# A gated cross-attention block: the second token half of the last batch gets a PSUM bank of its own, ScalarE scales it and VectorE adds it

## What is computed

```
x = x + tanh(g_xattn) * xattn(layernorm(x), ctx)          # attention over the context
x = x + tanh(g_ffn)   * ffn(layernorm(x))

ffn(x): gate = gelu(fp8(x) @ fp8(w_gating[0]))
        up   =      fp8(x) @ fp8(w_gating[1])
        return fp8(gate * up) @ fp8(w_linear)
```

## Time and profile before

| what | value |
|---|---|
| median of 3 runs | 49.52 us (49.23 to 51.98) |
| the profiled execution | 49.34 us |
| its span in the trace | 47.5 us |
| around the span | 1.84 us |
| PE busy | 41.6 us, 87% |
| DVE busy | 34.7 us, 73% |
| ACT busy | 29.5 us, 62% |
| POOL busy | 16.8 us, 35% |

### The profile page before, as it was taken

The page is one execution under the profiler, slowest core; times in us unless marked ns, Lnnn a source line. Parts: engine busy times, 40 slices in busy tenths (PEclk is TensorE's granted clock), DMA queues, the critical chain, the costliest instruction groups (busy, mean ns, idle before and its releaser), DMA issues.

```text
span 47.5 us, 841 instructions
## 1 busy us (share of the span) xinstructions
PE 41.6 (87%) x246; PEld 28.6 (60%) x246; DVE 34.7 (73%) x110; ACT 29.5 (62%) x67; POOL 16.8 (35%) x35
## 2 busy tenths in 40 slices
PE   3998999963999999998999999999999999999000
PEld 1317788833787888863435556665645888895000
DVE  0101099999798979899999991787669977999700
ACT  0902947299798799755599749775557495463000
POOL 3204994039999641600610170000000059802300
PEclk9999999999999999999999999999999999999999
DMA  0499999999999960000000000000000001460092
GB/s 0 79 365 326 317 367 369 195 203 203 170 114 104 106 61 1 0 0 21 0 0 0 0 0 0 0 0 7 0 0 0 0 14 64 163 215 0 0 340 102
DMA packets 3460, 4.64 MB, mean 98 GB/s; under 512 B 384, under 2 KB 2176, under 8 KB 3456
## 3 DMA queue, kind: packets, MB, share of 16 engines
q1 hardware_dynamic: 2304, 3.48, 21.5%
q0 software_dynamic: 864, 0.79, 17.7%
q10 hardware_dynamic: 288, 0.33, 2.2%
HBM read 5.90 MB, written 1.05 MB: 146 GB/s over the span
## 4 chain that ended last, share of the span: by engine, by line
PE 65%; DVE 13%; DMA 9%; ACT 2%; SPq 2%; issue 1%; DVEq 1%
PE bank L645 15%; PE bank L639 15%; PE bank L599 14%; PE bank L664 13%; DMA x_sb<-x 9%; DVE st L413 6%; PE bank L571 4%; DVE nmax L420 2%; PE bank L621 2%; DVE yo L486 2%; DVE mv L416 2%; PE bank L564 2%; SPq L211 2%; DVE attn L431 1%; ACT xq L344 1%; ACT ys L402 1%
## 5 line engine op out<-in xcount | busy, mean ns | idle before, releaser
L471 DVE SCALAR_TENSOR_TENSOR ap<-bank,gl 128x512 f16<-128x512 f32 (+1 forms) x20 | 11.6, 582 | 3.4 <-PE bank L645 1.8
L353 ACT ACTIVATE gl<-bank 128x512 bf16<-128x512 f32 (+1 forms) x20 | 10.0, 509 | 5.5 <-PE bank L639 5.4
L639 PE MATMUL bank<-xq,wg 128*128 128x512 fp8e4 (+1 forms) x40 | 10.2, 337 | 0.2 <-ACT xq L344 0.2
L645 PE MATMUL bank<-xq,wg 128*128 128x512 fp8e4 (+1 forms) x40 | 10.2, 337 | 0.0
L664 PE MATMUL bank<-wl,aq 128*128 128x256 fp8e4 x64 | 9.6, 273 | 0.0
L599 PE MATMUL bank<-attnT,xT_sb 128*128 128x256 f32 x32 | 8.1, 385 | 0.0
L664 PEld LDWEIGHTS bank<-wl,aq 128*128 128x128 f16 x64 | 6.2, 98 | 2.4 <-DVE aq L480 0.2
L280 POOL TENSOR_TENSOR yo<-ys,x 128x256 f32<-128x256 f32 x4 | 2.8, 730 | 10.3 <-ACT ys L361 10.3
L599 PEld LDWEIGHTS bank<-attnT,xT_sb 128*128 128x128 f32 x32 | 5.6, 190 | 0.7 <-ACT attnT L327 0.2
L265 POOL TENSOR_TENSOR r<-ve,neg_half 128x2 f32<-128x2 f32 x4 | 3.0, 760 | 8.5 <-DVE ve L454 8.5
L480 DVE TENSOR_SCALAR aq<-ap 128x512 uint16<-128x512 uint16 (+1 forms) x20 | 5.8, 292 | 0.0
(11 more groups left out here) (50 smaller groups left out, 54.4 us busy)
## 6 DMA issues: line engine op xcount, KB each, us to landing
x_sb<-x SPq DMA_DIRECT2D x4, 256.0 KB, 4.6
xT_sb<-xT SPq DMA_DIRECT2D x4, 256.0 KB, 7.1
out<-yo SPq DMA_DIRECT2D x5, 128.0 KB, 1.7
wg<-w_gating POOLq DMA_DIRECT2D x4, 128.0 KB, 8.6
par<-params_ctxT SPq DMA_DIRECT2D x1, 256.0 KB, 3.2
wl<-w_linear POOLq DMA_DIRECT2D x2, 128.0 KB, 11.0
out<-yo SPq DMA_DIRECT2D x1, 256.0 KB, 2.0
par<-params_ctxT SPq DMA_DIRECT2D x1, 194.0 KB, 2.9
```

The costliest lines, as they stand in the source:

```text
L353: nc.scalar.activation(gl[:, s % 2, toks], gate_b[s % 2][:, toks], ACT.Gelu_apprx_tanh).then_inc(gelu_ready, 1)
L471: nc.vector.scalar_tensor_tensor(ap[:, s % NAP, toks], up_b[s % 2][:, toks], ACT_SCALE, gl[:, s % 2, toks], ALU.mult, ALU.mult).then_inc(p ...
L639: mm = nc.tensor.matmul(gate_b[s % 2][:, toks], wg8[:, c, k, 0, o:o + P], xq[:, g, k, toks], start=(k == 0), stop=(k == KC - 1))
L645: mm = nc.tensor.matmul(up_b[s % 2][:, toks], wg8[:, c, k, 1, o:o + P], xq[:, g, k, toks], start=(k == 0), stop=(k == KC - 1))
```

## The change

The half (3, 1), second token half of batch 3, adds up in bank 0 instead of the second half of bank 7. Bank 0 is the one that batch 0's sums used. So the first matmul of ffn2(8) for that half, the fourth of four, now waits until ACT has scaled batch 0 out of bank 0, and scale_out(0) moves one place forward on ACT, from behind gelu(13) to behind gelu(12). At the end ACT scales the half (3, 1) into ys, and DVE adds x2 to it from there, instead of finish(3, 1).

```diff
-    OUT_AT = (HT + 5, HT + 6)
+    OUT_AT = (HT + 4, HT + 6)
...
         y_b = [bank[0:2], bank[6:8]]
+
+        def y_half(b, t):
+
+            return halves(bank[0] if (b, t) == (B - 1, LT - 1) else y_b[b // GB][b % GB])[:, t]
...
             act.wait_ge(ffn2_done, last_step(2) + 1)
             nc.scalar.activation(ys[:, 2, 1], halves(y_b[1][0])[:, 1], ACT.Copy,
                                  scale=yscale[:, 0:1]).then_inc(scaled_ready, 1)
+            act.wait_ge(ffn2_done, S)
+            nc.scalar.activation(ys[:, 3, 1], y_half(3, 1), ACT.Copy,
+                                 scale=yscale[:, 0:1]).then_inc(scaled_ready, 1)
 
             act.wait_ge(y_ready, 2)
             act.dma_start(out[3, :, 0], yo[:, 3, 0]).then_inc(s_out, 16)
...
             def finish(b, t):
-                g, i = divmod(b, GB)
                 dve.wait_ge(ffn2_done, last_step(b) + 1)
-                nc.vector.scalar_tensor_tensor(yo[:, b, t], halves(y_b[g][i])[:, t], yscale[:, 0:1],
+                nc.vector.scalar_tensor_tensor(yo[:, b, t], y_half(b, t), yscale[:, 0:1],
                                                x2[:, b, t], ALU.mult, ALU.add).then_inc(y_ready, 1)
...
             dve.wait_ge(scaled_ready, GB + 1)
             finish(2, 0)
             finish(3, 0)
-            finish(3, 1)
+            dve.wait_ge(scaled_ready, GB + 2)
+            nc.vector.tensor_tensor(yo[:, 3, 1], ys[:, 3, 1], x2[:, 3, 1], ALU.add).then_inc(y_ready, 1)
...
-                    mm = nc.tensor.matmul(halves(y_b[g][i])[:, t], aq[:, s % NAQ, m:m + P], wl8[:, j],
-                                          start=(j == 0 and t == 0), stop=(j == HT - 1), skip_group_check=True)
+                    apart = (GB * g + i, t) == (B - 1, LT - 1)
+                    if apart and j == 0:
+                        pe.wait_ge(scaled_ready, 1)
+                    mm = nc.tensor.matmul(y_half(GB * g + i, t), aq[:, s % NAQ, m:m + P], wl8[:, j],
+                                          start=(j == 0 and (t == 0 or apart)), stop=(j == HT - 1), skip_group_check=True)
```

## The result

| | before | this |
|---|---|---|
| median of 22 runs | 49.53 us (49.15 to 51.98) | 49.73 us (49.32 to 50.36) |
| ratio to before | 1 | 1.0078, 95% interval 1.0053 to 1.0103 |
| the profiled execution | 49.34 us | 49.55 us |
| its span | 47.5 us | 47.8 us |
| first feed-forward matmul, in the trace | 22.17 us | 22.20 us |

What follows compares the result with a forecast made beforehand. PE's unbroken chain from ffn2(8) was taken to bound the kernel, with transfers behind it. The 0.15 us wait, all else hidden, was added to the profiled 49.34 us for 49.5 us; 8-in-10 range 49.2 to 49.9.

Steps and rivals of the forecast that it cites:

- What bounds the kernel: From ffn2(8) at 37.72 to 42.97 us PE runs without idle time, so a delay there goes whole to the end.
- The new wait: ffn2(8)'s fourth matmul waits on PE for scale_out(0): a stall of 0.15 us, bounds 0.08 and 0.26.
- The upper bound's assumption: The fourth matmul's weight load also stands behind the wait, adding one matmul distance of 0.11 us, for a 0.26 stall.
- The earlier scaling: On ACT, scale_out(0) ahead of gelu(13) delays gelu(13) from 37.54 to at latest 37.98 us, at no cost.
- GpSimd's earlier adds: POOL's adds begin at 38.06 instead of 38.58 us and meet DVE's rounds; costs nothing, with 0.30 us left before up(16).
- the hold that was expected: On DVE, round(12) at about 38.8 us meets POOL's adds and is held to at most 39.55; no cost.
- the shut-out of VectorE by GpSimd: Rival: round(12) held until POOL's fourth add ends, up(16) waits 1.26 us on PE; 50.75 us, chance 0.03.
- The tail: ACT scaling then DVE add of (3, 1) end 0.05 to 0.11 us later, hidden behind the last store's 0.6 queueing.
- The rival in which load and last store are both exposed: Stall of 0.26 on PE plus last store hanging on DVE's end, 0.11 later: 49.71 us, chance 0.20.
- the sum's last line: Profiled execution 49.34 + 0.15 = 49.5 us, called as large as the median of the runs shown, 49.52.
- 2% is about what a measurement can tell: For the whole kernel, about 2%, 1.0 us, is distinguishable from no change; within 2% got 0.94, slower 0.04.

Runs made afterwards that it cites:

- The run with two scalings: The full change with batch 0's scaling run twice on ScalarE, the first copy into a tile nothing reads; profiled 50.47 us, ratio 1.0184.
- the run with the early scaling alone: The kernel before with only scale_out(0) one place forward on ScalarE; profiled 49.96 us, end 27.16 us from gate(0).
- the matmul later and the new tail: The full change with ffn2(8)'s waiting matmul issued one step later, ahead of ffn2(9); ACT scaling and DVE add kept; ratio 0.9967.
- the two runs with later stores: The kernel before with one or two extra VectorE instructions ahead of finish(3, 1); profiled 49.52 and 49.42 us, ends 27.17 and 27.38.
- the run with its wait and the old tail: The full change, but VectorE finishes (3, 1) in one instruction out of bank 0 as before; profiled 49.29 us, ratio 1.0027.
- the other two sets: The full change repeated unaltered, ratio 1.0044, and the change with finish(3, 1) in one VectorE instruction as before, ratio 1.0027.
- the four that should equal it: Matmul one step later with the change's or before's ending of (3, 1); before with early scaling; before with last store 0.4 later: ends 27.16 to 27.20.
- the three with the wait: The full change, its unaltered repeat, and the change with finish(3, 1) in one VectorE instruction as before: ends 27.35, 27.35 and 27.36 us.
- matmul later, new tail, split store: The full change with the waiting matmul one step later and batch 2's store cut in two; profiled 48.94 us, ratio 0.9976.

## Why the prediction was wrong

**What bounds the kernel: right.** The chain ran on PE without slack from ffn2(8) on. The run with two scalings, 0.56 us more wait and 0.59 us more time, shows it directly.

**The new wait: right in kind, too small.** The term was 0.15 us and measured 0.19 (0.18 at the end), inside its bounds of 0.08 and 0.26. The same steps with the measured numbers: ffn2(7) ends at 37.30; ACT follows after 0.04 instead of 0.02; the scaling takes 0.69 instead of 0.68; PE's matmul follows after 0.06 (38.03 to 38.09) instead of 0.05. Two hand-overs and one duration, each 0.01 or 0.02 short, add up to the missing 0.04. The 0.02 was read from a single hand-over of a chain, 42.97 to 42.99; in this place it takes twice that. The upper bound's assumption, that the load waits and then costs a whole distance more, did not come true: the load does wait (38.07), but the matmul is at 38.09.

**The earlier scaling: right.** gelu(13) starts at 37.92, and the run with the early scaling alone ends at 27.16 against 27.17.

**GpSimd's earlier adds: nothing paid, but the hold that was expected did not happen.** The timelines of VectorE and GpSimd in the changed kernel (line 487 rounds, line 284 adds):

```profile
38.73 0.22 DVE L487 TENSOR_SCALAR aq<-ap 128x256 uint16<-128x256 uint16 x1
...
39.43 0.22 DVE L487 TENSOR_SCALAR aq<-ap 128x256 uint16<-128x256 uint16 x1
...
40.30 0.22 DVE L487 TENSOR_SCALAR aq<-ap 128x256 uint16<-128x256 uint16 x1
```

```profile
38.10 0.72 POOL L284 TENSOR_TENSOR yo<-ys,x 128x256 f32<-128x256 f32 x1 [9.82 <-ACT ys L365]
...
38.78 0.74 POOL L284 TENSOR_TENSOR yo<-ys,x 128x256 f32<-128x256 f32 x1
...
39.66 0.72 POOL L284 TENSOR_TENSOR yo<-ys,x 128x256 f32<-128x256 f32 x1
```

The reader is to see that each round takes its plain 0.22. Each starts within the last 0.1 us of an add (the adds end at 38.82, 39.52 and 40.38), and round(12) starts 0.05 ahead of the next add as well (38.73 and 38.78). The prediction had put round(12) at 38.8, behind the start of the second add at 38.76, and so held to 39.55. It came 0.07 earlier, since gelu(13) began at 37.92 and not at the 37.98 that was its latest start, and it passed.

So the shut-out of VectorE by GpSimd did not happen; a round that comes on the other side of an add's start is not tested in the change itself. In two other runs round(13) was held: with the early scaling alone it lasted 0.37, and with the matmul later and the new tail 0.42:

```profile
39.63 0.42 DVE L487 TENSOR_SCALAR aq<-ap 128x256 uint16<-128x256 uint16 x1
```

Those kernels end at 27.16 and 27.20, within 0.03 us of before: a round that is longer by 0.15 or 0.20 us costs nothing there, as the prediction had worked out for a held round(12).

**The tail: right to the number.** The add was priced at 0.42 and took 0.42; the last store was to be 0.05 later beyond the wait, and is. It was to be hidden with 0.6 us to spare; the two runs with later stores measured 0.57. GpSimd's add of (2, 1) ends at 43.85 + 0.73 = 44.58 and the new add begins at 44.70, so the two did not meet. What the Trainium skill (SBUF — State Buffer, Who interferes with whom) says of two SBUF inputs was therefore not put to the test by any run here. The rival in which load and last store are both exposed, 49.71 us, comes closest to the measured median of 49.73, but by accident: neither of its two costs was paid.

**The step that failed** is the sum's last line: 49.34 + 0.15 = 49.5, "as large as that median". The wait was priced at 0.15 us and found to be paid in full, and that is a forecast of slower. But it was added to the one profiled execution, which was 0.18 us below the median of 49.52, and the result was set beside that median as if the two were comparable. The 0.18 hid the 0.15. Added to the median, the same working gives 49.52 + 0.15 = 49.67, and with the measured wait 49.52 + 0.19 = 49.71; the median measured is 49.73. The second half of the failure is the sentence that 2% is about what a measurement can tell: with 22 runs of each kernel the interval was 0.25% to either side, and in the other sets 0.33 to 0.56%. Against a limit of 2%, a wait of 0.15 us (0.3%) that was found to be paid in full could pass for no change.

**What stays open.** The size of the loss in the timed runs. The traces of the change show 0.18 us, twice, and 0.19 in the run with its wait and the old tail; the first ratio says 0.26 to 0.51 us (0.53% and 1.03% of 49.53). The same runs give 0.20 by the medians of all 22, and 0.16 by the means in the section on the result; so the first ratio is probably too large, and by how much is not shown. The ratios of the other two sets, 1.0044 and 1.0027, are compatible with 0.18, but neither interval excludes 1. I found no second cause in the trace: with the wait gone, the end returns to within 0.03 us of before. The traces carry the account; the timed runs alone would not settle 0.18 us.

## What to carry to other kernels

Where a new sum goes into a bank that still holds an old result, its first matmul waits for whoever empties the bank. Where PE is the chain, that wait costs its full length (0.19 us of wait, 0.18 at the end), even if the engine that empties the bank has time; here it was avoided by issuing that one matmul a step later. An instruction that is split over two engines gains nothing where the second part is nearly as long as the whole was and has to wait for the first (0.47 and 0.42 in a row against 0.48). And a small term is to be added to the same base with which it is compared: the difference is the forecast, not the sum.

## What the runs showed of the hardware that was not expected

- **How much executions differ before the change begins.** In the 13 profiled executions the first feed-forward matmul starts between 21.93 and 23.04 us. The rest agrees within 0.04 us among kernels whose later part is alike (27.16 to 27.20 for before and the four that should equal it, 27.35 to 27.36 for the three with the wait). In the chain of waits a part of this spread stands at the first loads: the piece that waits for x is 4.24 us long in the kernel before, 4.71 in the run with the matmul later and the new tail, 3.96 in the fastest profiled execution. Here one trace, counted from a common event, resolved 0.18 us, which 12 timed runs did not.

The three pieces, one fence for each kernel (before; matmul later, new tail; matmul later, new tail, split store):

```profile
1.64 4.24 DMA x_sb<-x
```

```profile
1.64 4.71 DMA x_sb<-x
```

```profile
1.63 3.96 DMA x_sb<-x
```

- **When a round is held by a GpSimd add.** In the change, rounds that start within the last 0.1 us of an add take 0.22 (38.73, 39.43 and 40.30), and the first of them starts 0.05 ahead of the next add's start at 38.78. In the kernel before, the round at 40.10 starts 0.11 behind an add's start and lasts 0.69, until 0.09 after that add's end; the one at 41.05, 0.43 long, also lasts until 0.09 after the end of its add. The add that the round at 40.10 meets:

```profile
39.99 0.71 POOL L280 TENSOR_TENSOR yo<-ys,x 128x256 f32<-128x256 f32 x1
```

Whether a round is held for most of an add hung on less than 0.2 us here, from 0.05 ahead of the add's start to 0.11 behind it. The prediction's start of round(12) was off by 0.07.
